# A graph kernel on one core: source rows of all parts in front of the second part's target rows, and the third layer's list in front of the second part's tiles

## The reference, cut to what matters

```python
for layer in (L0, L1, L2, L3):
    h = jnp.maximum(_layernorm(x, axis=-1), 0.0)
    x = x + layer(h, src, dst, ...)
```

```python
x = h[src]; y = h[dst]; c = w_comp[etype]
xb = jnp.einsum('ei,bio->ebo', x, weight)         # 16 bases, 32 x 32
msg = jnp.einsum('eb,ebo->eo', c, xb)
x_hat = x @ A1_w.T + A1_b
y_hat = y @ A2_w.T + A2_b + rel_emb[etype]
a = jnp.tanh(jax.nn.relu(jnp.sum(x_hat * y_hat, axis=-1) / scale))
nei = jax.ops.segment_sum(a[:, None] * msg, dst, num_segments=N)
```

## Time and profile before

| | us |
|---|---|
| median of 3 runs | 2741.11 |
| profiled execution, its own time | 2739.09 |
| its span | 2737.3 |
| DVE busy | 1731.8 (63%) |
| POOL busy | 1796.4 (66%) |
| PE busy | 430.9 (16%) |
| ACT busy | 341.8 (12%) |

### The profile page before, as it was taken

One profiled execution on the slowest core, in us unless ns is written; L12 is line 12 of the kernel. 1 busy time (PEld: TensorE's weight loads), 2 busy tenths in 40 slices (PEclk: granted clock), 3 DMA queues, 4 the chain that ended last, 5 costly groups with the idle time before them and its releaser, 6 DMA issues.

```text
span 2737.3 us, 12492 instructions
## 1 busy us (share of the span) xinstructions
PE 430.9 (16%) x2105; PEld 214.0 (8%) x2105; DVE 1731.8 (63%) x2937; ACT 341.8 (12%) x1043; POOL 1796.4 (66%) x1786
## 2 busy tenths in 40 slices
PE   0000000000001000000000097293294000016000
PEld 0000000000001000000000032031131000016000
DVE  8998897987129978278996078487888820420000
ACT  0000022111000110011211043141142200000000
POOL 6566677777742473577777656756556777466776
DMA  1001022221000131112210100100000210000000
GB/s 20 15 10 26 14 61 51 51 68 32 12 7 4 62 129 25 33 47 86 51 34 14 10 2 6 10 2 6 6 7 8 87 40 10 29 11 10 8 8 8
DMA packets 68011, 76.87 MB, mean 28 GB/s; under 512 B 34800, under 2 KB 60873, under 8 KB 67193
## 3 DMA queue, kind: packets, MB, share of 16 engines
q0 software_dynamic: 56384, 23.45, 6.5%
q1 hardware_dynamic: 5720, 27.38, 2.6%
q10 hardware_dynamic: 5856, 25.60, 2.5%
HBM read 35.67 MB, written 46.87 MB: 30 GB/s over the span
## 4 chain that ended last, share of the span: by engine, by line
DVE 45%; issue 27%; POOL 11%; PE 7%; another core or an unknown queue 5%; DMA 2%; ACT 1%; DVEq 1%; ACTq 0%; SPq 0%; POOLq 0%
POOL out L1573 9%; DVE mf L521 4%; DVE psum L903 3%; DVE psum L918 3%; DVE z L521 3%; DVE pay L521 2%; DVE outs L521 2%; PE psum L2017 2%; DVE pay L904 2%; PE psum L2018 2%; POOL mf L1567 1%; DVE psum L550 1%; DVE psum L913 1%; DVE xs L908 1%
## 5 line engine op out<-in xcount | busy, mean ns | idle before, releaser
L1567 POOL DMA_INDIRECT xs<-in_x,i_src x196 | 200.8, 1025 | 134.4 <-issue 56.4
L1567 POOL DMA_INDIRECT xd<-x_rows,i_dstX x196 | 195.9, 1000 | 128.5 <-DVE z L1377 93.9
L1567 POOL DMA_INDIRECT xd<-in_x,i_dst x196 | 205.1, 1046 | 109.3 <-DVE mf L521 47.5
L1573 POOL DMA_INDIRECT out<-outs,i_outS x196 | 200.7, 1024 | 112.7 <-issue 41.4
L1567 POOL DMA_INDIRECT mf<-x_rows,i_srcX x196 | 207.5, 1059 | 72.1 <-issue 72.1
L1573 POOL DMA_INDIRECT out<-outs,i_srcX x196 | 196.7, 1003 | 69.3 <-issue 58.9
L1567 POOL DMA_INDIRECT pay<-payload_by_dst,i_rank x196 | 195.2, 996 | 62.9 <-issue 62.9
L521 DVE TENSOR_TENSOR pay<-psum,pay 128x512 f32<-128x512 f32 x196 | 132.4, 688 | 117.5 <-ACT pay L1895 59.5
L521 DVE TENSOR_TENSOR mf<-mf 128x128 f32<-128x128 f32 (+5 forms) x578 | 175.7, 342 | 10.4
L2017 PE MATMUL psum<-pay 64*128 64x512 f16 x196 | 117.6, 600 | 183.6 <-ACT pay L1880 96.3
L1377 DVE TENSOR_REDUCE z<-pay 128x512 f32 (+1 forms) x196 | 132.4, 676 | 0.0
(11 more groups left out here) (458 smaller groups left out, 2398.4 us busy)
## 6 DMA issues: line engine op xcount, KB each, us to landing
z<-in_x ACTq DMA_DIRECT2D x14, 624.0 KB
out<-z ACTq DMA_DIRECT2D x14, 624.0 KB
l_first_rows<-mf SPq DMA_DIRECT2D x2, 3234.0 KB
outs<-in_x ACTq DMA_DIRECT2D x6, 624.0 KB
out<-outs ACTq DMA_DIRECT2D x6, 624.0 KB
l_own_rows<-pay SPq DMA_DIRECT2D x1, 3626.0 KB, 11.1
payload_by_dst<-z SPq DMA_DIRECT2D x1, 3234.0 KB
x_rows<-z SPq DMA_DIRECT2D x1, 3234.0 KB
```

The costliest lines, as they stand in the source:

```text
L1567: G.indirect_dma_start(out=dest(k), out_offset=None, in_=table, in_offset=bass.IndirectOffsetOnAxis(ap=idx[:, k:k + 1], axis=0), bounds_ch ...
L1573: G.indirect_dma_start(out=table, out_offset=bass.IndirectOffsetOnAxis(ap=idx[:, k:k + 1], axis=0), in_=source(k), in_offset=None, bounds_ ...
```

## The change

POOL: behind part 0's rows, the source rows of part 1 and of part 2 are issued first. The first 60 go at once, the other 60 one for each tile of turns 0. Then the 64 target rows of part 1, paced by the list's chain, a row every 1.5 links. Then the 56 target rows of part 2, one for each tile of turns 1. Then the sends: 20 free, 56 one for each tile of turns 2, the other 120 without a wait.

DVE: the list, with both `pointers` in front of it, stands ahead of `l2_inputs(1)`. PE: the list's products stand behind turn 18 instead of turn 34. No instruction that computes is added or removed.

```diff
-ROWS_FREE = (0, 60, 50)
-SENDS_LISTING, SENDS_FREE, SENDS_BESIDE = 40, 20, 56
+ROWS_FREE = 60
+SENDS_FREE, SENDS_BESIDE = 20, 56
@@ DVE
             pointers(1)
-            l2_inputs(1)
-            l2_turns(*L2_TURNS[1])
             pointers(2)
             marks["ends"] = link.n
             link(V.tensor_copy(icols["l3"][:], col("kn")))
             compact_edges(col("kn"), col("own"), wt, EDGES["l3"])
             marks["ended"] = link.n
+            l2_inputs(1)
+            l2_turns(*L2_TURNS[1])
             l2_inputs(2)
@@ POOL
-            for part, (lo, hi) in enumerate(L2_PARTS):
-                ahead = 0
-                for dest, idx, landed in ((lambda k: XY[:, k, 0:X2W], "srcX", "x2src_in"), (lambda k: XDW[:, k, :], "dstX", "x2dst_in")):
-                    for k in range(lo, hi):
-                        if part > 0 and ahead >= ROWS_FREE[part]:
-                            done = min(4 * L2_TURNS[part - 1][0] + ahead - ROWS_FREE[part], 4 * L2_TURNS[part][0])
-                            pool.wait_ge(s["l2_done"], 2 + done)
-                        gather(dest, x2_dram, icols[idx], last[P * EC], s[f"{landed}{part}"], 1, k)
-                        ahead += 1
+            for k in range(*L2_PARTS[0]):
+                source_row(0, k)
+            for k in range(*L2_PARTS[0]):
+                target_row(0, k)
+            for part in (1, 2):
+                for k in range(*L2_PARTS[part]):
+                    behind = k - L2_PARTS[1][0] - ROWS_FREE
+                    if behind >= 0:
+                        pool.wait_ge(s["l2_done"], 3 + behind)
+                    source_row(part, k)
+            for k in range(*L2_PARTS[1]):
+                pool.wait_ge(s["dve"], min(marks["ends"] + 3 * (k - L2_PARTS[1][0] + 1) // 2, marks["ended"]))
+                target_row(1, k)
+            for k in range(*L2_PARTS[2]):
+                pool.wait_ge(s["l2_done"], 2 + 4 * L2_TURNS[1][0] + k - L2_PARTS[2][0])
+                target_row(2, k)
...
-                    beside = k - SENDS_LISTING - SENDS_FREE
-                    if k < SENDS_LISTING:
-                        pool.wait_ge(s["dve"], min(marks["ends"] + 5 * (k + 1) // 2, marks["ended"]))
-                    elif 0 <= beside < SENDS_BESIDE:
+                    beside = k - SENDS_FREE
+                    if 0 <= beside < SENDS_BESIDE:
                         pool.wait_ge(s["l2_done"], 2 + 4 * L2_TURNS[2][0] + beside)
@@ PE
-            split = L2_TURNS[2][0] // 2
+            split = L2_TURNS[1][0] // 2
```

More of the change, by code:

```diff
@@ L1656, in _, with source_row, target_row @@
             pool.wait_ge(s["s_final"], 1)
-            for part, (lo, hi) in enumerate(L2_PARTS):
-                ahead = 0
-                for dest, idx, landed in ((lambda k: XY[:, k, 0:X2W], "srcX", "x2src_in"), (lambda k: XDW[:, k, :], "dstX", "x2dst_in")):
-                    for k in range(lo, hi):
-                        if part > 0 and ahead >= ROWS_FREE[part]:
-                            done = min(4 * L2_TURNS[part - 1][0] + ahead - ROWS_FREE[part], 4 * L2_TURNS[part][0])
-                            pool.wait_ge(s["l2_done"], 2 + done)
-                        gather(dest, x2_dram, icols[idx], last[P * EC], s[f"{landed}{part}"], 1, k)
-                        ahead += 1
+            def source_row(part, k):
+                gather(lambda q: XY[:, q, 0:X2W], x2_dram, icols["srcX"], last[P * EC], s[f"x2src_in{part}"], 1, k)
+            def target_row(part, k):
+                gather(lambda q: XDW[:, q, :], x2_dram, icols["dstX"], last[P * EC], s[f"x2dst_in{part}"], 1, k)
+            for k in range(*L2_PARTS[0]):
[14 more added lines that the diff above has]
+                target_row(2, k)
             pool.wait_ge(s["dense_out"], 16 * (DCHUNKS + 1))
```

## The result

The changed kernel took 2805.75 us (median of four, 2801.76 to 2810.76) against 2741.97 before (2739.32 to 2743.0): ratio 1.0235, 95% interval 1.0214 to 1.0256. Slower by 64 us, where 29.5 were forecast. The profiled execution has a span of 2807.0 us, against 2737.3.

A forecast was written before the change was run, and what follows sets the result against it. Dense POOL rows were taken to slow engines meeting new code, and POOL to bound the end behind the turns. Terms -31.9 + 10 + 51.4 = +29.5 gave 2771 us against the median; own range 2759 to 2790 (0.72), wider 2750 to 2806.

The forecast's parts named there:

- Turns of part 0, 0: Layer-2 turns of part 0: the 60 free rows beside their start stay, and with them the 68.9 us lost.
- Turns of part 1, -31.9: Layer-2 turns of part 1: nothing runs free at their start, so the whole loss of 31.9 us should go.
- from the second pass of the loop on it doesn't care: Turns: POOL issuing without a pause slows only engines meeting code for the first time, not later passes.
- The list, +10: Layer-2 list: dense POOL rows slow some 17 short instructions at its end; +10 us taken, about half of 18.
- The upper bound (+98.7): Layer-2 list: at most the whole difference between the first layer's list and this one, 169.8 - 71.1 us.
- The sends, +51.4: Behind part 2's turns: 40 more sends start where POOL is the bound, 1.28 us each, with nothing to hide them.
- Target rows in time: Target rows of parts 1 and 2: DVE waits for none; part 1's land with 10 us of cover.
- A: Rival: part 1's loss stays because it belongs to the loop's first pass itself; 2803 us, chance 0.12.
- B: Rival: the list's short instructions come at 1.40 us from its start, +98.7 instead of +10; 2860 us, chance 0.06.
- C: Rival: ScalarE's slow supply ends early and part 0's turns give back up to 68.9 us; 2702 us, chance 0.05.
- D: Rival: the sends are hidden where DVE or another stage is later, gain and loss cancel; 2741 us, chance 0.05.
- the port lock: Beside the list: VectorE's two-port modes would hold POOL's rows, DVE waiting 78 us; the prediction went by no wait.

The follow-up runs named there:

- the paced list: Changed kernel with a target row beside the list every 2.5 links instead of 1.5: 2802.02 us, ratio 1.0213 to before.
- memsets: Changed kernel with the 20 free sends held until part 1's turns end and 90 POOL memsets in their place: 2800.04 us, ratio 1.0207 to before.
- five sends: Kernel before with 70 sends beside part 2's turns instead of 56, five for four tiles: ratios 0.9928, 0.993 and 0.9998 on three chips.
- the first experiment: Changed kernel with the 20 free sends waiting until the last tile of part 1's turns is done: 2790.24 us, ratio 1.0173 to before.

## Why the prediction was wrong in size

The spans differ by 69.7 where 29.5 were forecast. Of the 40.2 between, part 1's turns bring 18.7, the list 16.8, part 0's turns 5.4 and the sends 2.3; 3.0 go back elsewhere.

*Turns of part 0, 0.* The term held but for 5.4 us, which come and go in the kernel before too.

*Turns of part 1, -31.9: came as -13.2.* The mechanism held. The chips that don't starve give these turns 116.9 us in a kernel that has them as before, against 116.4 worked out from part 2; and 117.6 with the sends held. What failed is the step "from the second pass of the loop on it doesn't care". I took it from before, where rows stopped running free early in a loop, so that the first pass and the dense rows always fell together, and it kept me from asking where the 20 free sends would go. The diff says it: 56 target rows for 64 tiles, then 20 free. The rest of the gain went there (135.1 - 117.6 = 17.5).

*The list, +10: came as +26.8.* The term was mis-sized by its choice of victims: the 17 short instructions at the end were to pay, the four long groups not. The third and the fourth group paid 13 and 16 us, the short instructions nothing. Whether DVE or PE was the one short of an instruction, the trace can't say; that it was the rows' density, the paced list shows. The upper bound (+98.7) held.

*The sends, +51.4: came as 53.7,* as argued: nothing hid them in after, on either kind of chip.

*Target rows in time:* right where the rows ran dense, and thin: the pause that cures the list makes DVE wait 20.6.

*The rivals.* A, part 1's loss stays for the loop's own sake, would have given 2803, and the time is near it, but not for its reason: the first passes ran clean. That the time lies just inside the wider range, 2750 to 2806, which A's term had opened, is therefore luck. The Trainium skill (Runtime: NRT & Kernel Launch, "Instruction fetch mechanics") would put such a stall at a taken branch; the same branches cost nothing on two chips and nothing beside memsets. A branch or a place in the code that costs only beside dense rows isn't excluded: with five sends the loss came once a pass. B, C and D didn't come. The rows beside the list took 63.25 / 64 = 0.99 us, so the port lock that the Trainium skill (SBUF — State Buffer, "Who interferes with whom") describes isn't to be seen there. Beside DVE's long instructions rows are held up: of the 20 sends beside `l2_inputs(2)` in the first experiment four took 1.46 to 2.60 us, and in before not one row but four of 21, 1.57 to 2.77 us.

Sum: +5.4 +26.8 -1.1 (inputs and the gaps between stages) -13.2 +53.7 -1.9 (behind) = 69.7.

## What to carry to other kernels

On two of the four chips a series of indirect DMAs without a pause is a cost for the engines that hand work to each other beside it: short copies and matmuls, but also the list's long groups with PE's products between. Put it beside a stage of few long instructions on one engine (27.5 us of inputs with 20 rows, no loss), and when a series is moved, find where each of its free pieces lands, not only where it left. A correlation in one profile (first pass and dense rows) isn't a cause until something separates them. And compare by stage: twice a total pointed to the wrong theory, and on other chips the same +2.4% was made of other terms.

## What the runs showed of the hardware

- The same program takes 2742 or 2751 us on two chips and 2500 on two others, at a granted clock of 1.00 in all profiles. The 242 us lie mainly in four places: 100 ahead of part 0's turns, 66 and 31 in the turns of parts 0 and 1, 44 behind `kc` in the third layer (stages of before on the first chip against those of the same code in the five-sends kernel on the third). In the turns they are the waits described above; that those ahead and behind are of the same kind isn't shown.
- A starved DVE runs one instruction every 1.40 us after some 20 at full speed, beside DMAs issued every 1.28 to 1.30 us. That the engines lack instructions is inferred from "issue" and "remote" alone, and the transfer of instructions from memory isn't seen to be slow. The profile of after lists the packets that bring them:

```profile
q14 instruction: 46, 0.38, 0.0%
q8 instruction: 4, 0.07, 0.0%
```

None took longer than 1.2 us, and the trace has none in the places that lost time: the packets next to the list's two waits start at 1712.66 and 1801.07, those next to the last 26 us of part 1's turns at 1842.86 and 1995.63, those next to the late scans at 1233.37 and 1279.08. Unless some are missing from the record, what is slow lies behind the transfer, in the engines or between them; what it is stays open.
- On these two chips, by run: 20 sends at 1.29 us cost part 1's last turns 17.5 us; 70 at 1.43 on the mean, in runs of some five without a pause, cost 24 us in 134; one row each 1.79 costs nothing, nor do 90 memsets in 29.75 us. The same spacing doesn't always cost: beside such rows the 32 scans of before took 3.3 us on one chip and 18.5 on another.
